# A residual block's side products in plain fp32 on halves of TensorE's rows, in place of f32r products on high and low parts

## The reference

```python
xn = _layernorm(x, axis=-1)
s = jnp.einsum('btd,dm->btm', xn, Win) + bin_          # 512 -> 64
h = jax.nn.relu(s[..., None] * W1 + b1)                # 64 -> 64 x 16
g = jnp.einsum('btmh,mh->btm', h, W2) + b2             # 64 x 16 -> 64
out = jnp.einsum('btm,md->btd', g, Wout) + bout        # 64 -> 512
x = x + attention(xn) + out
```

## Time and profile before

| | us |
|---|---|
| median of 3 runs | 374.67 |
| lowest and highest | 374.19, 376.34 |
| profiled execution | 375.8 |
| its span, first to last instruction | 373.7 |
| PE, DVE, ACT, POOL busy | 337.0, 282.9, 278.2, 237.3 |

### The profile page before, as it was taken

The page is one execution under the profiler, slowest core; times in us unless marked ns, Lnnn a source line. Parts: engine busy times, 40 slices in busy tenths (PEclk is TensorE's granted clock), DMA queues, the critical chain, the costliest instruction groups (busy, mean ns, idle before and its releaser), DMA issues.

```text
span 373.7 us, 5638 instructions
## 1 busy us (share of the span) xinstructions
PE 337.0 (90%) x1964; PEld 161.1 (43%) x1964; DVE 282.9 (76%) x507; ACT 278.2 (74%) x366; POOL 237.3 (64%) x209
## 2 busy tenths in 40 slices
PE   2489889789997998898999999999999999999774
PEld 2274554345533553444444444444434444443322
DVE  0677757888788799987969687877878787877664
ACT  0363568785786677867998999998989898988820
POOL 8405385992767649839094949494949585769900
PEclk9999989999999999999999999999999999999998
DMA  8999303334346425653575757576756652223647
GB/s 254 266 383 348 117 3 113 112 114 125 157 168 227 153 100 198 224 170 128 216 275 205 263 205 269 203 260 224 280 211 249 224 224 114 113 114 140 208 157 296
DMA packets 15052, 73.02 MB, mean 195 GB/s; under 512 B 4121, under 2 KB 4273, under 8 KB 6833
## 3 DMA queue, kind: packets, MB, share of 16 engines
q1 hardware_dynamic: 12304, 72.23, 53.1%
q0 software_dynamic: 640, 0.16, 0.8%
q10 hardware_dynamic: 2080, 0.28, 0.8%
HBM read 38.96 MB, written 33.69 MB: 194 GB/s over the span
## 4 chain that ended last, share of the span: by engine, by line
PE 63%; POOL 10%; DVE 8%; ACT 6%; issue 5%; DMA 5%; SPq 1%; POOLq 0%; DVEq 0%; ACTq 0%
PE op L443 14%; PE T L377 14%; PE g L425 13%; PE s L387 12%; POOL o L867 7%; DMA o<-in_L_attn_Wv_dram 5%; PE rep L410 4%; ACT H L541 3%; DVE stats L788 2%; PE g L396 1%; POOL rstd L842 1%; DVE o L763 1%; ACT G L551 1%; PE op L276 1%; DVE SH L774 1%
## 5 line engine op out<-in xcount | busy, mean ns | idle before, releaser
L867 POOL TENSOR_TENSOR o<-x,bias_row 128x512 f32<-128x512 f32 x128 | 164.1, 1319 | 4.0 <-issue 4.0
L541 ACT ACTIVATE H<-rep,b1c,w1c 128x1024 f32<-128x1024 f32 x128 | 153.6, 1206 | 14.5 <-PE rep L410 13.7
L763 DVE TENSOR_TENSOR o<-o,op 128x512 f32<-128x512 f32 x128 | 86.9, 682 | 39.3 <-PE op L443 38.3
L513 ACT ACTIVATE xT<-T 128x512 f32<-128x512 f32 x128 | 76.2, 596 | 39.7 <-PE T L377 39.2
L377 PEld LDWEIGHTS T<-ident,x 128*128 128x128 f32 x512 | 54.9, 142 | 107.4 <-issue 75.9
L377 PE MATMUL T<-ident,x 128*128 128x128 f32 x512 | 84.9, 289 | 11.6 <-DMA x<-in_L_attn_x_dram 9.1
L788 DVE BATCH_NORM_STATS2 stats<-x 128x6 f32<-128x512 f32 x128 | 83.2, 682 | 0.4
L842 POOL TENSOR_TENSOR rstd<-veps,nhalf 128x8 f32<-128x8 f32 x16 | 26.4, 1651 | 83.9 <-DVE veps L798 83.9
L387 PE MATMUL s<-xT,win 128*64 128x512 f32 x256 | 70.5, 630 | 0.0
L425 PE MATMUL g<-H,w2s 128*32 128x512 f32 x512 | 68.2, 605 | 0.4 <-ACT H L541 0.4
L443 PE MATMUL op<-wout_hi,G 128*128 128x512 f32 x128 | 62.7, 490 | 5.9 <-DVE G L781 3.7
(11 more groups left out here) (166 smaller groups left out, 246.5 us busy)
## 6 DMA issues: line engine op xcount, KB each, us to landing
x<-in_L_attn_x_dram SPq DMA_DIRECT2D x32, 1024.0 KB, 6.8
out_dram<-o SPq DMA_DIRECT2D x32, 1024.0 KB, 4.3
o<-in_L_attn_Wq_dram SPq DMA_DIRECT2D x1, 1024.0 KB, 14.6
o<-in_L_attn_Wk_dram SPq DMA_DIRECT2D x1, 1024.0 KB, 16.4
o<-in_L_attn_Wv_dram SPq DMA_DIRECT2D x1, 1024.0 KB, 19.4
o<-in_L_attn_Wo_dram SPq DMA_DIRECT2D x1, 1024.0 KB, 19.2
H<-in_L_ffn_Wout_dram SPq DMA_DIRECT2D x2, 128.0 KB, 14.7
bias_row<-in_L_ffn_bout_dram SPq DMA_DIRECT2D x1, 256.0 KB, 12.1
```

The lines of the kernel that those rows point to most:

```text
L513: act.activation(xT[:, c, b * BLK:(b + 1) * BLK], T_ps[k % 2][:, :], ACT.Copy).then_inc(ev_done, 1)
L541: act.activation(Hr[half][k % len(Hr[half])][:, :], rep_ps[:, :], ACT.Relu, bias=b1c[:, half, k:k + 1], scale=w1c[:, half, k:k + 1]).then_ ...
L763: dve.tensor_tensor(o_sb[m][:, c], o_sb[m][:, c], product_bank(n, j), ALU.add).then_inc(add_done, 1)
L867: pool.tensor_tensor(o_sb[m][:, c], x_sb[m][:, c], bias_row[:, :], ALU.add).then_inc(xc_done, 1)
```

## The change

The replication and the projection become plain fp32 products. Each contracts over only 64 rows, so the two halves of the data sit on partitions 0 to 63 and 64 to 127 and their products are given to the two halves of the array's rows (`tile_position=(b * M, 0)`), each into a bank of its own. The high and low parts of s, G and Wout and their instructions go: s_full and G are used as they are, in two buffers each. Two groups of 128 rows of x (even and odd) make one projection, so there are four projections a block, in every other slot, and DVE adds 1024 columns at a time. o_ps becomes two banks in one buffer; `A_ps` is now the second T bank, so up to slot 56 the transposes have one bank. The table of slots is: SPREAD 9 to 8, replication 13 and 17 to 11 and 15, g product 19 to 17, G 23 and 24 to 21, projection 25 to 22, add 26 to 23.

```diff
-        VARIANCE, INV_STD, SPREAD, COPY_R, SCALE, HIGH, LOW = 5, 6, 9, 9, 10, 11, 12
-        REPLICATE, RELU, SUM_H, G_HIGH, G_LOW, PROJECT, ADD, BIAS = (13, 17), 13, 19, 23, 24, 25, 26, 10
-        BODIES = N + 4
+        VARIANCE, INV_STD, SPREAD, COPY_R, SCALE = 5, 6, 8, 8, 10
+        REPLICATE, RELU, SUM_H, G_MADE, PROJECT, ADD, BIAS = (11, 15), 11, 17, 21, 22, 23, 10
+        TILES = TPP // 2
+        BODIES = N + 3
...
-        A_ps = o_ps[1]
+        A_ps = T_ps[1]
...
+        def every_other(t, first):
+
+            at = due(t, first, SLOTS)
+            return (at[0], at[1] // 2) if at and at[1] % 2 == 0 else None
...
             for b in range(2):
-                cols = slice(b * BLK, (b + 1) * BLK)
-                mm = pe.matmul(rep_ps[:, cols], spread[:, half, :], SH[:, cols], start=True, stop=True)
+                own = slice(b * M, (b + 1) * M)
+                mm = pe.matmul(rep_ps[:, b * BLK:(b + 1) * BLK], spread[own, half, :], s_full[n % 2][own, :],
+                               start=True, stop=True, tile_position=(b * M, 0))
             mm.then_inc(rep_done, 1)
...
-            for part in (wout_hi, wout_lo):
-                mm = pe.matmul(product_bank(n, j), G[m][:, j * P:(j + 1) * P], part[:, :], start=(part is wout_hi), stop=(part is wout_lo))
+            for b in range(2):
+                own = slice(b * M, (b + 1) * M)
+                mm = pe.matmul(o_ps[:, b * D:(b + 1) * D], G[n % 2][own, j * P:(j + 1) * P], wout[own, :],
+                               start=True, stop=True, tile_position=(b * M, 0))
             mm.then_inc(op_done, 1)
...
-        def g_high(n):
-            m = n % RING
+        def evacuate_g(n):
             if n == 0:
                 act.wait_ge(in_ffn, 16 * 12)
             act.wait_ge(g_done, HK * n + HK)
-            for b in range(2):
-                own, _, cols = halves(b)
-                act.activation(G[m][own, cols], g_ps[own, :], ACT.Identity, bias=b2c[own, 0:1]).then_inc(hi_done, 1)
+            act.activation(G[n % 2][:, :], g_ps[:, :], ACT.Identity, bias=b2c[:, 0:1]).then_inc(g_made, 1)
...
-            m, c = n % RING, slice(j * D, (j + 1) * D)
-            dve.wait_ge(op_done, SLOTS * n + j + 1)
-            dve.wait_ge(xc_done, SLOTS * n + j + 1)
-            dve.tensor_tensor(o_sb[m][:, c], o_sb[m][:, c], product_bank(n, j), ALU.add).then_inc(add_done, 1)
+            m, c = n % RING, slice(2 * j * D, (2 * j + 2) * D)
+            dve.wait_ge(op_done, TILES * n + j + 1)
+            dve.wait_ge(xc_done, SLOTS * n + 2 * j + 2)
+            dve.tensor_tensor(o_sb[m][:, c], o_sb[m][:, c], o_ps[:, :], ALU.add).then_inc(add_done, 1)
...
-        def s_low(n):
-            for b in range(2):
-                own, other, cols = halves(b)
-                dve.wait_ge(sh_done, 2 * n + b + 1)
-                dve.tensor_tensor(SH[other, cols], s_full[own, :], SH[own, cols].bitcast(F32), ALU.subtract).then_inc(sl_done, 1)
-
-        def g_low(n):
```

More of the change, by code:

```diff
@@ L67, in residual_block @@
         xT = sb("xT", [P, DC, PAIR])
-        s_full = sb("s_full", [P, BLK])
-        SH = sb("SH", [P, PAIR], F32R)
+        s_full = [sb(f"s_full{r}", [P, BLK]) for r in range(2)]
         Hr = [[sb(f"H{a}{i}", [P, PAIR]) for i in range(n)] for a, n in enumerate((HK, 3))]
-        G = [sb(f"G{r}", [P, PAIR], F32R) for r in range(RING)]
+        G = [sb(f"G{r}", [P, BLK]) for r in range(2)]
         stats = sb("stats", [P, TPP, 6])
@@ L137, in residual_block @@
         att = vn
-        A_ps = o_ps[1]
-        banks = [rep_ps[:, 0:D], rep_ps[:, D:2 * D], o_ps[0][:, :]]
+        A_ps = T_ps[1]
+        banks = [rep_ps[:, 0:D], rep_ps[:, D:2 * D], o_ps[:, 0:D], o_ps[:, D:2 * D]]
         NB = len(banks)
@@ L370, in transpose @@
             m, (c, b) = n % RING, divmod(k, 2)
[L371 to L377, removed]
+            if k == 0:
+                for h in range(2):
+                    pe.wait_ge(ld[m][h], 16 * (n // RING + 1))
+            t = SLOTS * n + k
+            if 0 < t <= T_ATT:
+                pe.wait_ge(ev_done, t)
+            elif t == T_ATT + 1:
+                pe.wait_ge(att_made, 1)
+            elif t > 0:
+                pe.wait_ge(ev_done, t - 1)
+            for j in range(TILES):
+                col0 = (2 * j + b) * D + c * P
+                mm = pe.transpose(turn_bank(n, k)[:, j * P:(j + 1) * P], x_sb[m][:, col0:col0 + P], ident[:, :])
             mm.then_inc(tr_done, 1)
@@ L393, in spread_rstd @@
             if n > 1:
-                pe.wait_ge(lo_done, 2 * (n - 1))
-            for j in range(4):
+                pe.wait_ge(g_made, n - 1)
+            for j in range(TILES):
                 mm = pe.transpose(g_ps[:, j * P:(j + 1) * P], rwide[:, j, :, :].rearrange("p b m -> p (b m)"), ident[:, :])
@@ L767, in scale_s @@
             dve.wait_ge(R_done, n + 1)
-            dve.tensor_tensor(s_full[:, :], s_ps[:, :], s_full[:, :], ALU.mult).then_inc(s_done, 1)
-        def s_low(n):
-            for b in range(2):
-                own, other, cols = halves(b)
-                dve.wait_ge(sh_done, 2 * n + b + 1)
-                dve.tensor_tensor(SH[other, cols], s_full[own, :], SH[own, cols].bitcast(F32), ALU.subtract).then_inc(sl_done, 1)
-        def g_low(n):
-            m = n % RING
-            for b in range(2):
-                own, other, cols = halves(b)
-                dve.wait_ge(hi_done, 2 * n + b + 1)
-                dve.scalar_tensor_tensor(G[m][other, cols], g_ps[own, :], b2c[own, 0:1], G[m][own, cols].bitcast(F32),
-                                         ALU.add, ALU.subtract).then_inc(lo_done, 1)
+            dve.tensor_tensor(s_full[n % 2][:, :], s_ps[:, :], s_full[n % 2][:, :], ALU.mult).then_inc(s_done, 1)
         def statistics(n, j):
```

82 lines of the change are left out of this document (28 added, 54 removed).

## The result

The changed kernel takes 426.4 us (median of 4, 424.4 to 428.5) where the kernel before takes 375.5: 1.135 times as long, 95% interval 1.130 to 1.139. The forecast was 415 us with a range of 391 to 452. In the late stage the kernel is slower for the forecast reasons; of the 11 us above the forecast, most lie at the start and in stretches at the lower clock.

What follows compares the result with a forecast made beforehand. PE's own list was taken to bound the kernel after the attention. +31 us there, +8 and +2 beside the attention and -1 at the end make +40 on 375.8; less 1.1, 415 us, range 391 to 452.

Steps and rivals of the forecast that it cites:

- the forecast reasons: After the attention: PE's longer list and new waits for G and relu, a body +3.5 us, +31 us in all.
- PE bounds the late stage: From 173 to about 332 us, time is PE's own list, 17.92 us a body; ACT and DVE savings are worth nothing.
- The pair at 0.86 + 0.2 us: Projection and replication: two fp32 products on row halves share the time, 0.86 us plus 0.2 to enter, 1.07 each.
- The list: PE's own work per late body: projection +0.7, replication +1.05, form changes -0.1 us, from 17.92 to 19.57.
- rival F: Load for a pair's second record waits for the first to end: 6 us more, 421 us; chance 0.08.
- The waits for G and relu: New PE waits per late body: 0.9 us before the projection for G's copy, 0.95 before the replication for relu.
- Beside the attention: Bodies while attention runs: +2 us for each of four bodies, +8, and +2 for the first three.
- most slots are longer than the loop of transpose and copy: Beside the attention, one T bank makes transposes wait for the previous copy; most slots exceed that loop (0.44 + 0.25 + 0.65 us).
- a danger for the late stage: After the attention, clock should stay at 1.00; longer stretches at 1.2 GHz would make the forecast too low.
- The end: After the last transposes: fewer relus and G parts against slower last products, -1 us, a guess between -4 and +3.

## Why the prediction was right, and where it was off

- **PE bounds the late stage: right.** All that ACT and DVE lost was worth nothing there, in the changed kernel and with the replication alone.
- **The pair at 0.86 + 0.2 us: right in sum.** A projection is 1.06 us ahead of g, and the transposes ahead of it take 0.59 to its start, 0.15 more than alone. The price of a pair's form was split otherwise than I had it: 0.15 us ahead of its start, 0.1 between its first and second records and 0.1 behind it, where I had 0.2 in and 0.14 out. The list came to 19.49 for 19.57. That halves of the rows share the time was taken from the products on halves of the columns; the run on the same rows shows it. The Trainium skill says that products on different tiles of the array run concurrently ("TensorE: Matmul & The Clock Gate", Part 3); here the trace agrees, with 1.06 us for a pair on two row groups and 1.91 on one. The load rule of the same part of the Trainium skill (rival F) is not borne out: with both products on the same rows the records follow at 0.43 us behind the first, loads and all, where open loads of 0.11 would make it 0.54. That the first load behind a change of form is open, which would be the 0.1 ahead of the second records, fits the rows (it starts together with the first record, at 273.91) but was not tested by a run of its own.
- **The waits for G and relu: right,** 0.83 and 0.96 for 0.9 and 0.95, and right in kind: moving G's copy and the projections took most of both away.
- **Beside the attention: the term that was too small.** I took +2 us for each of bodies 3 to 6 and +2 for the first three together. Bodies 3 to 6 grew by 10.5 us (1.4, -0.1, 3.7 and 5.5), the first three by 5.7. In bodies 2 to 6 PE's waits that DVE ended went down from 8.5 to 7.0 us, as I had credited; those that ACT ended went up from 2.0 to 8.6, and these I had priced only in part. My words that most slots are longer than the loop of transpose and copy pass over the slots with transposes alone. Some 4 us of the 16.2 belong to the clock, by estimate. In body 6, from 182.1 to 192.3 us, it cost 2.6: L365 took 3.6 us where it takes 1.9 and the replication 1.9 for 1.1, while ahead of L365 nothing was lost, as PE waited for DVE there (L365 starts 24.1 us after the body's first transpose here and in the run with the second half of x ahead of Win, which was at full clock until then). In body 1, PE was busy for 6.5 us at half the clock and in the kernel before for 3.4, which makes 1.6. That clock I had named as a danger for the late stage, not priced.
- **A term that was left out: +4.4 us at the start.** The diff shows that a block's first transposes wait for both halves of x; I read past it. The kernel before with this wait alone loses 3.4 us.
- **The end: -1 forecast, +2 measured.** The products and adds are 2.45 us apart, as reckoned (2.6). The lower clock adds 0.9 us to each of the last three, 2.8 in all, which the run with work in the waits takes away again; without it the end would be the -1 forecast.
- **The sum of the misses.** They add up: +4.4, +6, -2 and +3 us make the 11 between 415 and 426. By cause, the start has 4.4 of them and the clock some 7 (4.2 and 2.8, an estimate); what is left, +2 in the first bodies and -2 in the late stage, cancels.

## What to carry to other kernels

When one engine's list is the bound, price a change by that list from start to start, then walk the slots for the places where the list gets thin: the engines behind it fall due there, and both new waits of this case stood right behind a slot with four transposes alone. A product that saves another engine's work but costs the bounding engine more is a loss however much it saves. Evenness can be worth more than the list: three ways of saving a forecast 0.5 to 1 us of PE's list were tried in the kernel before, whose second engine was busy for 91% of a body. They saved 0, 0.2 and 0.7 us of PE's busy time and cost 2.0, 1.0 and 1.3 in waits. And where a change makes the bounding engine wait, price the lower clock as well: here it is the larger part of the miss.

## What the runs showed of the hardware that was not expected

- Two fp32 products of 64 x 128 x 512 on the two halves of the rows are 1.06 us ahead of the next form, and 1.91 on the same half, so sharing one half costs 0.85 us.
- Behind a change of form the second record of a product follows the first later than the 0.43 us that records of one form keep: by 0.53 us in the projection (weights of 128 columns), 0.48 in s (64) and 0.46 in g (32). The surplus, 0.10, 0.05 and 0.03 us, falls with the columns of the weights. The rows of g and s:

```profile
261.05 1.06 PE L432 MATMUL g<-H,w2s 128*32 128x512 f32 x8
261.51 0.61 PE L432 MATMUL g<-H,w2s 128*32 128x512 f32 x4
262.05 1.08 PE L393 MATMUL s<-xT,win 128*64 128x512 f32 x4
262.53 0.60 PE L393 MATMUL s<-xT,win 128*64 128x512 f32 x2
```

- s after g, both on parts of the columns but 64 and 32 wide, costs as much as leaving for the transposes: 1.00 us from g to s, 1.01 from s to the transposes, where two s steps in one group take 1.87.
- In the last waits of 1.3 us, an extra fp32 product in each went with a granted clock of 1.00 up to the last add's end and a stretch 2.8 us shorter; 0.27 us of each wait was left. It is one execution.
